# Four edits of order and place in the second attention layer's aggregation stage of a graph network

## The reference, cut to what matters

```python
def gat_conv(x, src, dst, W, a_src, a_dst, b, num_nodes):
    h = einsum('nd,dhf->nhf', x, W)
    logits = leaky_relu(sum(h * a_src)[src] + sum(h * a_dst)[dst], 0.2)
    e = exp(logits - segment_max(logits, dst)[dst])
    z = segment_sum(e, dst)
    alpha = e / (z[dst] + 1e-16)
    return segment_sum(h[src] * alpha[..., None], dst).reshape(num_nodes, -1) + b

h   = gat_conv(x, src1, dst1, W1, a_src1, a_dst1, b1, n)      # loops appended to the edges
out = gat_conv(h, src1, dst1, W2, a_src2, a_dst2, b2, n)
x   = _layernorm(x + out)
```

## Time and profile before

| | |
|---|---|
| median of the runs | 3865.31 us (3860.82 to 3867.19) |
| the profiled execution | 3845.83 us |
| its span, first to last instruction | 3844.1 us |
| instructions | 56581 |
| TensorE matmul busy | 3249.5 us, 85% of the span |
| VectorE busy | 2816.0 us, 73% |
| GpSimd busy | 2085.0 us, 54% |
| ScalarE busy | 1883.4 us, 49% |
| all DMA queues | 684.76 MB, 178 GB/s over the span |
| this stage, first load's issue to the last norm | 1028.56 to 1261.17 us of the span |

### The profile page before, as it was taken

How to read it: one execution, slowest core, us unless ns; L and a number is a source line. 1 busy time by engine, 2 the same in 40 slices (tenths; PEclk the granted TensorE clock), 3 DMA queues, 4 the chain that set the end, 5 groups by cost and what they waited for, 6 DMA issues and landing times. The chain is left out here.

```text
span 3844.1 us, 56581 instructions
## 1 busy us (share of the span) xinstructions
PE 3249.5 (85%) x14868; PEld 2617.9 (68%) x14868; DVE 2816.0 (73%) x7894; ACT 1883.4 (49%) x5403; POOL 2085.0 (54%) x2118
## 2 busy tenths in 40 slices
PE   5999925588577799666999997999999999999875
PEld 4888824477465466333777775888878787878664
DVE  5666758699588466695666665898989898989742
ACT  3777715466333111132333332566666666666555
POOL 3667600376277566233333332767767676767567
PEclk8999969899799899755999998999999999999998
DMA  4788739644277222175333333887868686868665
GB/s 139 242 247 248 237 108 321 194 131 129 68 219 208 87 88 87 30 219 157 101 115 108 118 107 98 239 236 212 251 201 251 198 250 203 252 200 248 198 215 167
DMA packets 677311, 684.76 MB, mean 178 GB/s; under 512 B 73152, under 2 KB 631284, under 8 KB 676896
## 3 DMA queue, kind: packets, MB, share of 16 engines
q1 hardware_dynamic: 592456, 484.44, 40.4%
q0 software_dynamic: 68160, 181.21, 17.4%
q10 hardware_dynamic: 16380, 15.49, 1.2%
HBM read 401.66 MB, written 283.11 MB: 178 GB/s over the span
## 5 line engine op out<-in xcount | busy, mean ns | idle before, releaser
L2812 PE MATMUL s_i_bank<-s_i_messages,s_i_equal 128*128 128x256 f32 x1200 | 360.0, 383 | 5.6 <-DMA s_i_messages<-h,table_row 5.4
L621 POOL DMA_INDIRECT s_i_messages<-h,table_row x300 | 306.5, 1022 | 98.5 <-issue 78.7
L621 POOL DMA_INDIRECT s_i_messages<-h,table_row_b x300 | 308.0, 1027 | 90.1 <-issue 79.7
L931 POOL TENSOR_TENSOR n_powers<-n_powers,neg_half 128x8 f32<-128x8 f32 (+3 forms) x164 | 268.4, 1637 | 160.2 <-DVE n_powers L896 116.1
L856 ACT ACTIVATE n_z<-gamma_bc,n_powers 128x256 f32<-128x256 f32 x320 | 175.0, 594 | 362.0 <-POOL n_powers L931 362.0
L815 PE MATMUL s_n_bank<-w,n_xt 128*128 128x256 f32 x1280 | 305.7, 382 | 16.7 <-DMA n_xt<-in_x_t 16.7
L833 PE MATMUL s_n_bank<-w_out,n_ht 128*128 128x256 f32 x1280 | 313.9, 390 | 4.7 <-ACT n_ht L843 4.4
L824 PE MATMUL s_n_bank<-n_x3t,w_in 128*128 128x256 f32 x1280 | 302.5, 379 | 0.0
L2841 DVE SCALAR_TENSOR_TENSOR s_i_y<-s_i_bank,s_i_scale,acc 128x256 f32<-128x256 f32 x600 | 285.1, 476 | 0.3 <-PE s_i_bank L2812 0.2
L833 PEld LDWEIGHTS s_n_bank<-w_out,n_ht 128*128 128x128 f32 x1280 | 249.0, 196 | 46.2 <-ACT n_ht L843 11.1
L815 PEld LDWEIGHTS s_n_bank<-w,n_xt 128*128 128x128 f32 x1280 | 245.2, 192 | 51.3 <-DMA n_xt<-in_x_t 17.1
(11 more groups left out here) (448 smaller groups left out, 9244.8 us busy)
## 6 DMA issues: line engine op xcount, KB each, us to landing
h<-s_i_y SPq DMA_DIRECT2D x600, 128.0 KB, 3.9
n_xt<-in_x_t SPq DMA_DIRECT2D x160, 256.0 KB
out<-n_w SPq DMA_DIRECT2D x160, 256.0 KB
s_i_equal<-eq_tab SPq DMA_DIRECT2D x600, 64.0 KB, 3.9
x<-s_x_rows SPq DMA_DIRECT2D x100, 256.0 KB
out<-s_a_hs SPq DMA_DIRECT2D x100, 128.0 KB, 3.0
proj_dst<-s_a_hd SPq DMA_DIRECT2D x100, 128.0 KB
h<-s_h_rows SPq DMA_DIRECT2D x50, 256.0 KB, 3.7
```

Source lines behind the costliest of these rows:

```text
L621: return net.nc.gpsimd.indirect_dma_start(out, None, table, bass.IndirectOffsetOnAxis(index, 0))
L931: self.nc.gpsimd.tensor_tensor(v[:, 8 + b0:8 + b1], v[:, b0:b1], self.net.neg_half[:, 0:b1 - b0], ALU.pow).then_inc(self.powered, 1)
L2812: nc.tensor.matmul(banks[r % 4][:, 0:D], EQ[q % NM][:], M[q % NM][:], start=True, stop=True).then_inc(summed, 1)
```

## The change

All of it is in `gat2`:

- TensorE's turn becomes `total(i)`, `transposes(i-1)`, `project(i-2)`; VectorE's begins with `weigh(i+1)` (weigh(0) is ahead of the loop); `EQ` has four buffers and its load waits for the sums of pair k-4 instead of k-3. SyncE's list of loads keeps its order.
- The first tile of a pair (g = 0) gets x and bias in the projection's accumulation: one more matmul of `X[:, 0, :]` by `spread`, which is the identity with ones in its whole row 0. Row 0 of `X[:, 0, :]` holds c12, put there once; the gather must not overwrite it, so it goes by a second index whose row 0 is out of the table, with a bounds check. The second tile keeps bias, add and `Y` as before. The first tile's statistics and its norm read PSUM. The projection has four PSUM buffers and waits for the norm of pair k-4 and for the gather.
- GpSimd's turn becomes `get(i+2)`, `power(i-3)`. The wait in `get` is the same line as before, and is now for the add of the second tile.
- End rows go straight to their place in `EF` by two DMAs a turn, without the table in memory, and L1901 is gone.
- Step k = N takes x and c12 by two matmuls.

```diff
-    G, NB = 2, 3
+    G, NB, NE = 2, 3, 4
     N = T // G
...
-        EQ = st.sb("d_equal", [P, G, P], n=NB)
+        EQ = st.sb("d_equal", [P, G, P], n=NE)
...
         Y = st.sb("d_y", [P, G, D], n=3)
...
         EF = st.sb("d_ends", [T, 2, D])
-        eq_in, o_in, x_in = (st.sem(f"d_{n}", NB) for n in ("eq_loaded", "out1_loaded", "x_gathered"))
+        spread = st.sb("d_spread", [P, P])
+        x_index = st.sb("d_x_index", [P, N], I32)
+        eq_in = st.sem("d_eq_loaded", NE)
+        o_in, x_in = (st.sem(f"d_{n}", NB) for n in ("out1_loaded", "x_gathered"))
         ends_out, stored = (st.sem(f"d_{n}", m) for n, m in (("ends_stored", 2), ("x1_stored", 3)))
...
-        sums, tps, prs = (st.ps(f"d_ps_{n}", 2) for n in ("sums", "t", "p"))
+        sums, tps, prs = (st.ps(f"d_ps_{n}", m) for n, m in (("sums", 2), ("t", 2), ("p", 4)))
...
         def _(sp):
             def load(k):
                 if k < N:
-                    past(sp, summed, k - NB + 1)
-                    sp.dma_start(EQ[k % NB][:], net.eq_tab[k * G:(k + 1) * G, :, :].rearrange("g p e -> p g e")).then_inc(eq_in[k % NB], 16)
+                    past(sp, summed, k - NE + 1)
+                    sp.dma_start(EQ[k % NE][:], net.eq_tab[k * G:(k + 1) * G, :, :].rearrange("g p e -> p g e")).then_inc(eq_in[k % NE], 16)
                     past(sp, agg_ready, k - NB + 1)
                     sp.dma_start(O[k % NB][:], tiles(net.out1, k)).then_inc(o_in[k % NB], 16)
             def store_ends(k):
                 if 0 <= k < N:
                     sp.wait_ge(agg_ready, k + 1)
-                    sp.dma_start(net.ends[k * G:(k + 1) * G, :, :].rearrange("g r d -> r g d"), A[k % 2][0:2, :, :]).then_inc(ends_out[k % 2], 16)
+                    for g in range(G):
+                        sp.dma_start(EF[k * G + g:k * G + g + 1, :, :], A[k % 2][0:2, g, :]).then_inc(ends_out[k % 2], 16)
             def store(k):
                 if 0 <= k < N:
...
             for i in range(TURNS):
                 load(i + 2)
                 store_ends(i - 1)
-                if i == N:
-                    for u in range(2):
-                        sp.wait_ge(ends_out[u], 16 * (N // 2))
-                    sp.dma_start(EF[:], net.ends[:, :, :]).then_inc(ends_in, 16)
                 store(i - 4)
         @block.gpsimd
...
                 if k < N:
                     for g in range(G):
                         t = k * G + g
-                        gather(net, X[k % NB][:, g, :], a["x"], net.index[:, t, 1:2]).then_inc(x_in[k % NB], 16)
+                        x_rows = bass.IndirectOffsetOnAxis(x_index[:, k:k + 1] if g == 0 else net.index[:, t, 1:2], 0)
+                        nc.gpsimd.indirect_dma_start(X[k % NB][:, g, :], None, a["x"], x_rows, bounds_check=net.N - 1, oob_is_err=False).then_inc(x_in[k % NB], 16)
                 if k == N:
...
+
+            gp.wait_ge(based, NB + 4)
             def power(k):
                 if 0 <= k <= N:
...
             for k in range(2):
                 get(k)
             for i in range(TURNS):
+                get(i + 2)
                 power(i - 3)
-                get(i + 2)
...
                 if k <= N:
                     past(pe, agg_ready, k - 1)
                     if k == N:
-                        pe.wait_ge(ends_in, 16)
+                        for u in range(2):
+                            pe.wait_ge(ends_out[u], 16 * G * (N // 2))
                         nc.tensor.matmul(sums[k % 2][0:T, 0:D], net.upper[:], EF[:, 0, :], start=True, stop=True).then_inc(summed, 1)
                     else:
                         pe.wait_ge(weighted_ready, k + 1)
                         for g in range(G):
...
             def transposes(k):
...
                 if 0 <= k <= N:
                     p, w = rows(k)
                     pe.wait_ge(xt_ready, k + 1)
-                    past(pe, y_ready, k - 1)
+                    pe.wait_ge(x_in[k % NB], 32 * (k // NB + 1) if k < N else 32 * (N // NB) + 16)
+                    past(pe, x1_ready, k - 3)
                     for g in range(w):
+                        out = prs[k % 4][0:p, g * D:(g + 1) * D]
+                        if k < N and g == 0:
+                            nc.tensor.matmul(out, spread[:], X[k % NB][:, g, :], start=True, stop=False)
+                        if k == N:
+                            nc.tensor.matmul(out, net.ident[0:T, 0:T], X[k % NB][0:T, 0, :], start=True, stop=False)
+                            nc.tensor.matmul(out, net.ones[0:1, 0:T], net.c12[0:1, :], start=False, stop=False)
                         for c in range(C):
-                            mm = nc.tensor.matmul(prs[k % 2][0:p, g * D:(g + 1) * D], XT[k % 2][:, c, g * P:g * P + p], net.w2[:, c, :], start=c == 0, stop=c == C - 1)
+                            mm = nc.tensor.matmul(out, XT[k % 2][:, c, g * P:g * P + p], net.w2[:, c, :], start=c == 0 and g == 1, stop=c == C - 1)
...
+            pe.wait_ge(based, NB + 4)
             for i in range(TURNS):
+                total(i)
                 transposes(i - 1)
                 project(i - 2)
-                total(i)
         @block.scalar
         def _(act):
...
                 if 0 <= k <= N:
                     p, w = rows(k)
                     act.wait_ge(shift, k + 1)
+                    past(act, stored[k % 3], 16 * (k // 3))
                     for g in range(w):
-                        mv = nc.scalar.activation(Y[k % 3][0:p, g, :], Y[k % 3][0:p, g, :], ACT.Identity, bias=S[k % 4][0:p, 22 + g:23 + g],
+                        y = prs[k % 4][0:p, 0:D] if g == 0 else Y[k % 3][:, 1, :]
+                        mv = nc.scalar.activation(Y[k % 3][0:p, g, :], y, ACT.Identity, bias=S[k % 4][0:p, 22 + g:23 + g],
                                                   scale=S[k % 4][0:p, 20 + g:21 + g])
                     mv.then_inc(x1_ready, 1)
             for i in range(TURNS):
...
             def weigh(k):
                 if k < N:
...
                     for g in range(G):
                         t = k * G + g
...
             def aggregate(k):
                 if 0 <= k <= N:
                     dve.wait_ge(summed, k + 1)
                     past(dve, tp_made, k - 1)
-                    past(dve, ends_out[k % 2], 16 * (k // 2))
+                    past(dve, ends_out[k % 2], 16 * G * (k // 2))
                     if k == N:
...
                     else:
...
             def bias(k):
+                if 0 <= k < N:
+                    dve.wait_ge(x_in[k % NB], 32 * (k // NB + 1))
+                    V.tensor_tensor(X[k % NB][:, 1, :], X[k % NB][:, 1, :], net.c12[:], ALU.add).then_inc(b_ready, 1)
+
+            def stats(k):
                 if 0 <= k <= N:
                     p, w = rows(k)
-                    dve.wait_ge(x_in[k % NB], 32 * (k // NB + 1) if k < N else 32 * (N // NB) + 16)
-                    V.tensor_tensor(X[k % NB][0:p, 0:w, :], X[k % NB][0:p, 0:w, :], net.c12[0:p, :].unsqueeze(1).broadcast_to([p, w, D]),
-                                    ALU.add).then_inc(b_ready, 1)
-
-            def join(k):
-                if 0 <= k <= N:
-                    p, w = rows(k)
-                    s, y = S[k % 4], Y[k % 3]
+                    s = S[k % 4]
                     ch = Chain(dve, chain, 2 * w + 1, 0)
                     ch.base = k * (2 * G + 1)
                     dve.wait_ge(projected, k + 1)
-                    dve.wait_ge(b_ready, k + 1)
-                    past(dve, stored[k % 3], 16 * (k // 3))
-                    V.tensor_tensor(y[0:p, 0:w, :], two(prs[k % 2])[0:p, 0:w, :], X[k % NB][0:p, 0:w, :], ALU.add).then_inc(y_ready, 1)
-                    dve.wait_ge(y_ready, k + 1)
                     past(dve, x1_ready, k - 3)
-                    for g in range(w):
-                        ch(V.bn_stats(s[0:p, 6 * g:6 * g + 6], y[0:p, g, :]))
+                    if k < N:
+                        dve.wait_ge(b_ready, k + 1)
+                        past(dve, stored[k % 3], 16 * (k // 3))
+                        V.tensor_tensor(Y[k % 3][:, 1, :], prs[k % 4][:, D:2 * D], X[k % NB][:, 1, :], ALU.add).then_inc(y_ready, 1)
+                    ch(V.bn_stats(s[0:p, 0:6], prs[k % 4][0:p, 0:D]))
+                    if k < N:
+                        dve.wait_ge(y_ready, k + 1)
+                        ch(V.bn_stats(s[:, 6:12], Y[k % 3][:, 1, :]))
                     ch.wait()
                     for g in range(w):
                         ch(V.bn_aggr(s[0:p, 12 + 2 * g:14 + 2 * g], s[0:p, 6 * g:6 * g + 6]))
...
                     ch(V.tensor_scalar(s[0:p, 18:18 + w], s[0:p, 12:12 + 2 * w:2], -1.0, None, ALU.mult))
                     V.tensor_scalar(s[0:p, 16:16 + w], s[0:p, 13:13 + 2 * w:2][:, 0:w], EPS, None, ALU.add).then_inc(var, 1)
                     ch.close()
+            for b in range(NB):
+                V.tensor_copy(X[b][0:1, 0, :], net.c12[0:1, :]).then_inc(based, 1)
+            V.tensor_copy(x_index[:], net.index[:, 0:T:G, 1]).then_inc(based, 1)
```

(26 more changed lines are left out.)

## The result

The changed kernel takes 4123.51 us (median of four runs, 4119.79 to 4128.36) against 3863.07 for the kernel before (3859.90 to 3867.19): a ratio of 1.0673, 95% interval 1.0657 to 1.0690. That is 260 us slower; 4140 had been forecast, in a range of 4070 to 4200. The profiled execution took 4119.79 us.

What follows compares the result with a forecast made beforehand. The prediction took a loop of waits through several engines to bound the stage. 43 turns lengthened from 4.23 to 10.34 us, two to 8.2, and 4 for the tail gave 275 us more: 4140 us, range 4070 to 4200.

Steps and rivals of the forecast that it cites:

- Present bound: In the stage before the change, a loop through several engines, not one full engine, sets the 4.21 us turn.
- "engines as limit" estimate: In the changed stage, a turn would take 3.5 us if only the engines limited it.
- The ring and its place: Gather, power, norm, store, load of equal, weigh, aggregate, bias now lead from one add to the next: 10.34 us a turn.
- Rival (a): Load of equal not in the ring; the store of x1 alone sets 8.2 us a turn, 4048 us; chance 0.08.
- (b): Rival: the ring does not close, TensorE's 3.51 us is the turn, 3830 us in all; chance 0.05.
- (c): Rival: no change, savings met by new waits, 4.2 us a turn; chance 0.03.
- (d): Rival: same ring but costlier, landing near 4.7 and gathers slowed, 12.0 us a turn, 4212 us; chance 0.06.
- The terms: The steps around the ring from one add to the next, summed to 10.34 us, bounds 9.2 and 12.0.
- Add to gather: From the add's start on VectorE to the first gather's start on GpSimd: 0.69 us with a 0.417 add.
- Landing of equal: Time from issue of the load of equal until it lands: 3.1 us, bounds 2.0 and 4.7.
- Counts and ends: 43 turns of the ring, two of 8.2 us by the store alone, start unchanged, tail 4 us longer.
- Savings and small costs: VectorE's bias and add 0.27 us less each, SyncE at most 0.36 more a turn, PSUM norm 0.05 either way.

Runs made afterwards that it cites:

- e3: Changed kernel with power before get on GpSimd and equal loaded one turn earlier: 3857.68 us, ratio 0.9986.
- e5: Changed kernel with power before get, equal loaded one turn earlier and a fourth buffer for Y: 3856.90 us, ratio 0.9976.
- e8: Kernel before with only the TensorE/VectorE reordering, equal one turn earlier into four buffers, four Y, power before get: 3863.68 us, ratio 0.9996.
- e9: Changed kernel with power before get, equal one turn earlier, four Y, plain gather first and a third aggregate buffer A: 3846.25 us, ratio 0.9953.
- e1: Changed kernel with GpSimd doing power(i-3) before get(i+2) again, all else as changed: 3913.01 us, ratio 1.0131.
- e2: Changed kernel with equal loaded one turn earlier in SyncE's list, GpSimd's order as changed: 4047.30 us, ratio 1.0479.
- e4: Kernel before with only get(i+2) moved ahead of power(i-3) on GpSimd: 4034.95 us, ratio 1.0447.
- e6: Changed kernel with tile 1 gathered first in plain form without bounds check, then tile 0 with the check: 4106.92 us, ratio 1.0622.
- e10: Kernel before with only the direct end rows, two small DMAs a turn into EF: 3864.41 us, ratio 0.9995.
- e7: Changed kernel with power before get, equal one turn earlier, four Y and the plain gather first: 3853.15 us, ratio 0.9963.

## Why the prediction was right

**Present bound.** Right: in the kernels with power first and equal early (e3, e5, e8, e9) the sums no longer stand in the aggregation's way. What its removal is worth was overrated in the "engines as limit" estimate (3.5 a turn): the rings through the store and the end rows and the landing of equal stood close behind it. The estimate counts none of them, and the ring through the end rows is named nowhere in the prediction.

**The ring and its place.** Right in both halves. e1 and e2 each take one edge out and find nearly the length the sum gives for what is left. For e1 that is 5.05 (10.1 over two turns), 5.2 with equal landing in a median of 2.77 where weigh waited; measured are 5.49 in the middle of the stage, and the last 0.3 stays open. For e2 it is the store ring, 8.0 to 8.4, and 8.23 are measured. e4 puts only the one edge in and gets 7.98. Rival (a), the ring by the store alone, falls with e2: there the turn dropped by 1.9, so the load was in the ring. (b) held for two turns at the start, where no power was behind a gather yet. (c) and (d) fall with the measured 10.13.

**The terms.** Forecast 10.34, measured 10.11 in the turn shown, but two misses cancel, and that the sum came so close is luck. Add to gather: 0.69 forecast, 1.22 measured, because the check's set-up was costed at 0.08 on the gather alone; e6 shows that the 0.53 belongs to it. The trace of before held it: the one checked gather (L1916) had an idle 0.9 before it, the plain one started 0.28 after the join's end (1142.51 + 0.68 to 1143.47). Landing of equal: 3.1 forecast, 2.43 measured (median of 44, from 2.27 to 3.05), close to the lone 2.2 of the earlier trace rows, so the store issued 0.41 before it costs little. That store lands early too: the add at 1496.58 came 2.25 after the issue of the store it waited for, at 1494.33, where the prediction had 2.9. By the rule of the Trainium skill ("DMA: Bandwidth & Descriptors", Queues, rings and completion order) equal should not report before that store; it reported a median of 2.84 after the store's issue, and never under 2.67, so the trace agrees and the rule did not bind. The lower end of 2.5 that the prediction worked out beside it does not hold, since it came from the 2.9. The other terms: gathers 2.41 (2.39), power 1.04 (1.11), norm 1.08 (1.12), store to load 0.41 (0.40), weigh 0.39 (0.40), aggregate 0.79, bias 0.33 (0.34).

**Counts and ends.** 43 and 2 turns were right. The two took 8.05 for 8.2, again by two misses that cancel: 0.53 more from add to gather, 0.65 less for the store's landing. The tail is 3.8 for 4, with TensorE waiting 15.1 us for the last small DMA before the sums of the end rows, as the prediction had it. The start was put at no change and gave 5.1 back. It is 20.0 to 21.0 us from the first load to add 2 in every kernel with the new order on TensorE and VectorE, e8 with that order alone among them, and 25.1 in e4 without it, as in the kernel before; e10, also without it, had 22.7, so part of it is open. In all: 9.0 for 43 turns of 0.21, 5.1 for the start, 0.5 for the two turns and the tail, and 2.2 because the forecast started from a median of 3865.31 and not 3863.07, which is 4140 against 4123.5. That its figure for the profiled execution, 4121, met 4119.79 is luck: the stage grew by 260 and not 275, and the other 14 lie outside it.

**Savings and small costs.** Bias 0.418 and add 0.418, statistics from PSUM 0.422 against 0.408 from the other tile, norm from PSUM 0.563 against 0.589: all as costed and all without effect. The two end-row issues take 1.17 us of SyncE against 0.33 for the one before, 0.84 more and not 0.36: a mis-sized term that was hidden here. The landing of these DMAs had no term at all, and the aggregation waited for it in e5 and e7. TensorE's clock fell to 0.72 without moving the turn, as the sum had it.

## What to carry to other kernels

Where every engine runs its own list, a step's place in its list is a dependency like any other: walk each loop of waits once around, through the lists as well, and divide its length by the number of turns it spans. Moving power one turn later on GpSimd and weigh one turn earlier on VectorE turned three turns into one, with VectorE and DMA idle two thirds of the time. What opens such a ring is a turn more to go around in: the old order on GpSimd was worth 210 us, the load one turn earlier alone 76. A faster instruction shortens it only by its own saving, 20 us here. And the next ring can be right behind: it was in e3, e5 and e7.

## What the runs showed of the hardware that was not expected

A gather with a bounds check started 0.80 us after the end of the add it waited for (0.79 to 0.82 in 44 turns of the changed kernel), a plain one 0.28 after (0.28 to 0.29 in 44 turns of e6); right behind another gather both followed 0.30 after its end. The 0.52 us between them is idle time of GpSimd in the trace and in no busy time. A DMA of two rows of 1 KB to one partition took SyncE 0.57 us to issue (median of 88), one of both tiles' end rows to memory 0.33.
